# A graph network's last pass picks rows by one-hot products, its first attention pass gets a ring of 28 groups, and its projection stages run three norms ahead

## The reference

```python
h = relu(layernorm(x)); x = x + log_softmax(sage2(h, src, dst))      # two SAGE convolutions
h = relu(layernorm(x)); x = x + gat_ff(h, src, dst)                  # 4 heads, batchnorm, feed-forward
h = relu(layernorm(x)); x = x + gat_prelu(h, src, dst)               # 2 heads
h = relu(layernorm(x))
msg = h[src] @ weight[rel] + bias[rel]                               # 4 relations
agg = where(deg > 0, segment_max(msg, dst), 0)
return x + h @ weight[-1] + bias[-1] + agg
```

## Time and profile before

| what | value |
|---|---|
| median of 3 runs | 5873.08 us |
| the profiled execution's own time | 5876.16 us |
| its span, first to last instruction | 5874.4 us |
| mean granted clock of TensorE | 0.728 |
| TensorE busy | 3278.1 us (56%) |
| VectorE busy | 2906.4 us (49%) |
| ScalarE busy | 1827.9 us (31%) |
| GpSimd busy | 3903.4 us (66%) |

### The profile page before, as it was taken

The page is one execution under the profiler, slowest core; times in us unless marked ns, Lnnn a source line. Parts: engine busy times, 40 slices in busy tenths (PEclk is TensorE's granted clock), DMA queues, the critical chain, the costliest instruction groups (busy, mean ns, idle before and its releaser), DMA issues. The chain is left out here.

```text
span 5874.4 us, 89970 instructions
## 1 busy us (share of the span) xinstructions
PE 3278.1 (56%) x15772; PEld 2756.8 (47%) x15773; DVE 2906.4 (49%) x7625; ACT 1827.9 (31%) x6493; POOL 3903.4 (66%) x4083
## 2 busy tenths in 40 slices
PE   3444555545555525889999894244555563334332
PEld 3444455444555523677777644233445533333331
DVE  4233344434455656788888852344555652222221
ACT  2111111111122213666666653233344441111110
POOL 4777777677777747777776003777777517777776
PEclk9667777766677756999999995566677785555555
DMA  4222222211111112344444211222222134444443
GB/s 122 61 62 63 63 65 66 72 53 52 53 53 52 53 41 78 111 113 117 119 117 113 95 46 31 52 53 54 53 53 52 38 111 130 133 132 130 131 133 107
DMA packets 441899, 474.71 MB, mean 81 GB/s; under 512 B 131954, under 2 KB 337214, under 8 KB 441695
## 3 DMA queue, kind: packets, MB, share of 16 engines
q0 software_dynamic: 130464, 264.37, 17.1%
q1 hardware_dynamic: 184116, 146.31, 8.3%
q10 hardware_dynamic: 127227, 63.09, 3.6%
HBM read 315.46 MB, written 157.97 MB: 81 GB/s over the span
## 5 line engine op out<-in xcount | busy, mean ns | idle before, releaser
L1194 PE MATMUL pa<-arena,weighted 128*128 x4480 | 860.0, 367 | 855.8 <-POOLq L913 511.2
L1194 PEld LDWEIGHTS pa<-arena,weighted 128*128 128x128 f32 x4480 | 795.4, 273 | 909.4 <-issue 909.2
L422 POOL DMA_INDIRECT arena<-y_tab,slot x784 | 739.8, 944 | 398.7 <-issue 209.4
L1607 POOL DMA_INDIRECT arena<-t_tab,src_idx x784 | 777.5, 992 | 265.7 <-issue 216.0
L919 POOL DMA_INDIRECT arena<-h_tab,src_idx x784 | 742.8, 947 | 308.1 <-issue 221.9
L2490 POOL DMA_INDIRECT arena<-t_tab,src_idx x784 | 753.3, 961 | 244.9 <-issue 224.6
L919 POOL DMA_INDIRECT arena<-sage_tab,src_idx x784 | 739.8, 944 | 262.4 <-issue 216.1
L471 DVE TENSOR_TENSOR_SCAN scan_t<-mask,scan_t,pa 128x512 f32<-128x512 bf16 x196 | 250.9, 1280 | 737.1 <-PE pa L495 737.1
L495 PE MATMUL pa<-ident,arena 128*128 128x128 f32 x784 | 218.3, 434 | 603.9 <-DMA arena<-y_tab,slot 603.9
L495 PEld LDWEIGHTS pa<-ident,arena 128*128 128x128 f32 x784 | 140.1, 217 | 681.9 <-DMA arena<-y_tab,slot 430.8
L2731 PE MATMUL pa<-weighted 128*128 128x130 f32 x2240 | 422.6, 364 | 21.0 <-ACT weighted L2809 11.0
(11 more groups left out here) (522 smaller groups left out, 6559.9 us busy)
## 6 DMA issues: line engine op xcount, KB each, us to landing
gat_tab<-out_rows SPq DMA_DIRECT2D x248, 260.0 KB
scan_rows<-out_rows ACTq DMA_DIRECT2D x196, 256.0 KB, 3.7
arena<-t_tab,src_idx POOLq DMA_INDIRECT x1568
mask<-cut_row SPq DMA_DIRECT2D x196, 128.0 KB, 3.1
arena<-h_tab,src_idx POOLq DMA_INDIRECT x784
arena<-sage_tab,src_idx POOLq DMA_INDIRECT x784
y_tab<-arena SPq DMA_DIRECT2D x49, 256.0 KB, 2.3
arena<-y_tab,slot POOLq DMA_INDIRECT x784, 2.8
```

The source lines that it names most:

```text
L422: nc.gpsimd.indirect_dma_start(out=rows(c, t), out_offset=None, in_=table[:, :], in_offset=bass.IndirectOffsetOnAxis(ap=slot[:, c, t:t + 1 ...
L1194: ins = nc.tensor.matmul(pa[:, b * CE:b * CE + RW], hot[b][:, t * P:(t + 1) * P], ring[:, bass.ds(start + t * RW, RW)], start=(t == 0), st ...
L1607: nc.gpsimd.indirect_dma_start(out=rows[:, g % QR * QT + t, :], out_offset=None, in_=t1_tab[:, :], in_offset=bass.IndirectOffsetOnAxis(ap= ...
```

## The change

**Last layer.** `edge_pass`, `gather_results`, `scan_rows` and `last_idx` go. In their place stands a walk of 160 steps over a ring of 8 groups of 7 tiles, filled from y_tab. Step s: ScalarE copies the group from the ring to `staged_t` (`stage_group`), TensorE transposes it (`turn`), VectorE scans 896 edges and carries the last value to the next step where that has the next group (`scan`), TensorE transposes back (`back`), ScalarE copies the result from PSUM (`keep_back`), and TensorE multiplies it by a one-hot matrix that is 1 where an edge is the last of its node (`select`), which puts each node's row on its partition. VectorE adds it to x (`add`), and ScalarE stores the block to the output (`store`); a block that several steps touch is stored by each. Masks are broadcast by ScalarE's queue (`load_mask`). The rows of last edges come from `last_rows`, made in the pass from dst_rows and gathered by group.

**First attention pass.** QR is 28. `arena` and `x` become one tensor `wide`, and the ring lies over x. x is stored to `x_tab` by SP in the projection stage in front of the pass, and loaded in the feed-forward stage behind it, ahead of the additions.

**Fronts.** In stages with `starts`, front(i+2) comes ahead of the wait for product i, as in the others.

**Small.** `group_col1` and `block_col1` keep the first attention pass from overwriting the others; three small operations, a transpose, a few memsets and the load of scan_rows go.

```diff
-QR = 17
+QR = 28
...
     def step(i, b, left):
-        if left > 1 and starts is None:
+        if left > 1:
             front(dve, i + 2)
         dve.wait_ge(group_product.sem, group_product.past(i + 1))
         post(dve, i, b)
-        if left > 1 and starts is not None:
-            front(dve, i + 2)
...
+                sp.dma_start(x_tab[...], x[:, i * NG:(i + 1) * NG, :]).then_inc(stored.sem, 16)
...
+                sp.dma_start(x, x_tab.rearrange("(j p) d -> p j d", p=P)).then_inc(x_here.sem, 16)
...
-        edge_pass(y_tab, D, y_idx, cut_row, ALU.add, ALU.max)
...
+    # SP
+    with sp.Fori(0, GN) as g:
+        n = sp.value_load(retire_walk[0:1, bass.ds(g, 1)], min_val=1, max_val=SN)
+        wait_apart(sp, edge_staged.sem, edge_staged.past(n))
+        sp.sem_inc(group_freed.sem, 1)
+    # VectorE
+    def scan(s, b):
+        after(dve, edge_turned, s + 1)
+        after(dve, mask_loaded[b], (s - b) * 8 + 16)
+        after(dve, edge_back, s - 1)
+        after(dve, carry_ready, s)
+        v.tensor_tensor_scan(run_t[b], mask_t[b], turned_ps[b], carry_t[b], ALU.add, ALU.max).then_inc(edge_scanned.sem, 1)
+        ... (two operations that make carry_t[1 - b])
+    def add(s, b):
+        after(dve, block_summed, s + 1)
+        after(dve, block_added, s)
+        after(dve, block_stored, s * 16)
+        v.tensor_tensor(row, row, last_ps[b], ALU.add).then_inc(block_added.sem, 1)
+    def body(i, b):
+        scan(i, b); build(i, b); add(i - 2, b)
+    # TensorE
+    def turn(s, b):
+        after(pe, edge_staged, s + 1)
+        after(pe, edge_scanned, s - 1)
+        ... (7 transposes of staged_t[b] to turned_ps[b])
+    def back(s, b):
+        after(pe, edge_scanned, s + 1)
+        after(pe, edge_kept, s)
+        ... (7 transposes of run_t[b] to back_ps)
+    def select(s, b):
+        after(pe, edge_kept, s + 1)
+        after(pe, hot_built, s + 1)
+        after(pe, block_added, s - 1)
+        ... (7 matmuls of hot[b] and kept_t[b] to last_ps[b])
+    def body(i, b):
+        turn(i + 1, 1 - b); select(i - 1, 1 - b); back(i, b)
+    # ScalarE
+    def stage_group(s, b, start, need):
+        after(act, edge_turned, s - 1)
+        wait_apart(act, group_landed.sem, group_landed.past(need))
+        nc.scalar.copy(staged_t[b]..., ring[...]).then_inc(edge_staged.sem, 1)
+    def load_mask(s, b, need):
+        after(act, edge_scanned, s - 1)
+        act.dma_start(mask_t[b], cut_row[...].broadcast_to([P, GE])).then_inc(mask_loaded[b].sem, 16)
+    def keep_back(s, b):
+        after(act, edge_back, s + 1)
+        after(act, block_summed, s - 1)
+        nc.scalar.copy(kept_t[b], back_ps).then_inc(edge_kept.sem, 1)
+    def store(s, b, j):
+        after(act, block_added, s + 1)
+        act.dma_start(out[bass.ds(j * P, P), :], x[:, bass.ds(j, 1), :]...).then_inc(block_stored.sem, 16)
+    def body(i, b):
+        keep_back(i, b); store(i - 2, b, j)
+        stage_group(i + 2, b, start, need); load_mask(i + 2, b, need)
```

More of the change, by code:

```diff
@@ L28 @@
 NB = 4
-CHUNKS = ET // CT
-ITERS = CHUNKS // NB
 H1, H2, R = 4, 2, 4
@@ L250, in build @@
         sums_ready = count("sums_ready")
[L252 to L259, removed]
+        iota_made = count("iota_made")
         table_in = count("table_in")
@@ L319, in build @@
         cuts_kept = count("cuts_kept")
[L320 to L325, removed]
+        edge_staged = count("edge_staged")
+        edge_turned = count("edge_turned")
+        edge_scanned = count("edge_scanned")
+        edge_back = count("edge_back")
+        edge_kept = count("edge_kept")
+        carry_held = count("carry_held")
+        carry_ready = count("carry_ready")
+        mask_loaded = [count(f"mask_loaded{b}") for b in range(2)]
         group_staged = count("group_staged")
@@ L564, in results_gathered @@
-        def results_gathered():
-            for b in range(2):
-                group_rows[b].base += 16 * NG * ((groups + 1 - b) // 2)
-            group_here.base += groups
         def stage(s):
@@ L583, in group_steps, with project @@
                 step(i, i % 2, min(groups - 1 - i, 2))
-        def project(ns, front, by_tile, by_group, post, begin=None, scalar_front=None, scalar_post=None, gathers=None, store=None,
+        def project(ns, front, by_tile, by_group, post, begin=None, scalar_front=None, scalar_post=None, store=None,
                     buffers=None, starts=None):
@@ L608, in project @@
             with nc.Block() as block:
-                if gathers is not None:
-                    @block.gpsimd
-                    def _(pool):
-                        gathers(pool)
                 if starts is not None:
@@ L1363, in _ @@
                 few = {"allow_slow_non_contiguous": True}
-                for c in (*hot_made, chunk_scanned, chunk_copied, *written, tile_out, group_kept, *tile_stored):
+                for c in (tile_out, group_kept, *tile_stored):
                     act.sem_inc(c.sem, c.ahead)
@@ L2886, in _ @@
             @block.vector
             def _(dve):
-                with dve.Fori(0, groups) as i:
-                    dve.wait_ge(group_here.sem, group_here.past(i + 1))
-                    nc.vector.tensor_tensor(middle(x, i), middle(x, i), middle(g, i), ALU.add).then_inc(group_kept.sem, 1)
-            @block.sync
-            def _(sp):
-                for i in range(groups):
-                    sp.wait_ge(group_kept.sem, group_kept.past(i + 1))
-                    j, full = i * NG, NG if i < groups - 1 else NG - 1
-                    sp.dma_start(out[j * P:(j + full) * P, :].rearrange("(j p) d -> p j d", p=P), x[:, j:j + full, :]
-                                 ).then_inc(stored.sem, 16)
-                sp.dma_start(out[(NT - 1) * P:N, :], x[0:NL, NT - 1, :]).then_inc(stored.sem, 16)
-                sp.wait_ge(stored.sem, stored.past(16 * (groups + 1)))
+                v = nc.vector
```

393 lines of the change are left out of this document (197 added, 196 removed).

## The result

The changed kernel takes 5946.05 us (median of 4 runs, 5939.82 to 5949.07) against 5872.95 for the kernel before on the same chip: ratio 1.0122, 95% interval 1.0105 to 1.0140: slower, clear of noise and by under 2%. The prediction said 5954 and gave slower a chance of 0.66. The profiled execution took 5939.82 us, with a span of 5938.1 and a mean granted clock of 0.779.

What follows compares the result with a forecast made beforehand. GpSimd's gathers were taken to pace the old last pass; in the new one TensorE and ScalarE alternate. Last pass +110 and fronts -29 give +81 on 5876.2, 5957, or 5954 against the median; range 5820 to 6105 us.

Steps and rivals of the forecast that it cites:

- The ring of two engines: Last pass: TensorE and ScalarE alternate by queue order, so a step costs the sum of both engines' work.
- Its price: One step of the last pass: 5.96 us at full clock, 9.07 at half clock.
- store's issue between the two copies: ScalarE's time for issuing the store between keep_back and stage_group: taken as 0.5 us, bounds 0.1 and 0.7.
- The clock: Last pass: granted clock 0.78 at TensorE busy near 0.63, paired from the earlier windows, giving 7.0 us a step.
- The gathers don't hold it: Last pass: the gather bound of 1136 us lies below the walk's 1168, with gathers priced 1.247 us apart.
- Sum of the pass: Last pass: 42 + 160 x 7.0 + 6 = 1168 us against 1058.4, +110 us.
- Fronts: Two projection stages: earlier fronts save 13 us in the first and 16 in the second, together -29 us.
- Ring of 28, store and load of x: First attention pass: larger ring gives 0 (bounds -25 and 0); moving x costs 0, at most 10 us.
- Full clock: Rival, chance 0.20: clock stays full in the last pass, step 5.96 us, gathers pace the first half; 5833 us.
- half clock: Rival, chance 0.08: half clock throughout the last pass, 9.07 us a step, +412; 6285 us.
- gathers as the sole pace: Rival, chance 0.03: gathers stay the last pass's pace, if the two engines' ring costs under 5.4 us; 5777 us.
- Mask or store late: Rival, chance 0.06: landings over 6 us make the last pass's steps about 8 us, +241; 6115 us.

Runs made afterwards that it cites:

- e3: The changed kernel with ScalarE's stage_group and load_mask moved ahead of keep_back and store; ratio 1.0274 to the kernel before, on a slow chip.
- e7: The changed kernel with TensorE's step reordered to turn, back, select; ratio 1.0235 to the kernel before, on a slow chip.
- e8: The changed kernel with ScalarE's stage copy made twice in each step; ratio 1.0629 to the kernel before, on a slow chip.
- e4: The changed kernel with the one-hot build's row of numbers in PSUM instead of SBUF; ratio 1.0440 to the kernel before, on a slow chip.
- e11: The changed kernel with TensorE's order turn, back, select and the build's row in PSUM; ratio 1.0327 to the kernel before, on a slow chip.
- e1: The kernel before with only the edit putting front(i+2) ahead of the wait for product i; ratio 0.9987 to the kernel before, on a slow chip.
- e2: The changed kernel with the first attention pass's ring back at 17 groups; ratio 1.0412 to the kernel before, on a slow chip.

## Why the prediction was right

- **The ring of two engines: right.** PE waits for the stage copy and ScalarE for back, in turn, as forecast; e3, e7 and e8 show that the order and the copies' length set the step. Of the signs one came only at the end: gathers stopped for the ring twice, 7.4 us in all. The eight slots took up what the walk fell behind until the last two groups.
- **Its price: 0.71 us too high at full clock** (5.25 against 5.96). The term "store's issue between the two copies", taken as 0.5 with bounds 0.1 and 0.7, measured -0.07: a bound from the earlier trace rows that did not hold, because there the issue waited for its copy and here it doesn't. The Trainium skill (TensorE: Matmul & The Clock Gate, Architectural detail) has ScalarE's queue eight deep and strict first in, first out, which allows that overlap; the trace agrees with it, and its case of 6.6 us a step is what the second half shows (6.61). The handoff back to TensorE, 0.23 from the earlier trace rows, measured 0.06 (5564.42 to 5564.48).
- **The clock: right, by a wrong pairing.** 0.77 and 0.78 in both halves against 0.78, but TensorE is 72% busy at 0.75 where the earlier trace rows had 59% at 0.75. The busy share alone doesn't fix the clock: e7 has 1.00 at 73% busy.
- **"The gathers don't hold it": wrong for the first 495 us.** They held 63 steps there, at 7.9 us each. The step of the sum that failed is the gathers' price of 1.247 us: they came 1.34 us apart (1052.4 / 783), as 65 us went into long ones (805.4 - 739.9).
- **Sum of the pass:** 494.4 to 5281, 641 to 5922 and 16.1 to the end are 1151.5, forecast 1168. The cheaper step (some 0.4 x 160 = -64) and the gathers' hold nearly cancel, so part of the hit is luck: with gathers of 1.247 and steps of 6.61 the pass would have come to 48 + 160 x 6.61 = 1106 or the gather bound's 528 + 86 x 6.61 + 6 = 1102, some 45 us less.
- **Fronts: right, -26.3 against -29.** First stage 8.1 against 13: the first post came 3.1 us later than the old (2099.01 against 2098.22 with 2.3 us of lead), forecast 2.5, and the period was 7.3 against 7.4, but the 49 scatters took 66.6 us from first to last (2100.06 to 2166.70), as six of them took 1.33 to 1.87, against 63. (The prediction's last paragraph has posts 9 us apart there, its sum 7.4; the sum was right.) Second stage 18.2 against 16: a period of 10 us against 10.8.
- **Ring of 28, store and load of x: 0, right.** The first attention pass with the feed-forward stage behind it is as long as before within 2 us (above), and the way from the first gather of the second attention pass to that of the last pass took 1151.2 us against 1152.0.
- **Rivals.** Full clock, half clock and gathers as the sole pace didn't happen. Mask or store late: VectorE's scan does wait 323.9 us for the mask's load, 157 times, but under TensorE's select; ScalarE waits only 10.0 us for a scan.

## What to carry to other kernels

Write both engines' queues side by side and follow one item through them: a copy that stands behind a wait for the other engine's last instruction makes the two take turns, whatever is double-buffered, and moving one call in either body takes it out (e3, e7). Price each thing in such a ring from a row where it has the same wait; where there is no such row, let its lower bound be 0. And before a stretch is put down to the chain of waits, check the period ahead of and behind the point at which it changes engines, and whether the engine that it blames was itself waiting there.

## What the runs showed of the hardware

- **A build with two operands in SBUF lengthens a gather's issue.** In the changed kernel 129 of the last pass's 784 gathers take 0.98 to 1.86 us, where the others take 0.944. Of these 129, 126 start while one of VectorE's builds runs, and each is longer by about what the build has left, less 0.1 us: the one at 5563.41 takes 1.61, 0.67 more, and the build had 0.78 us to go. Of the gathers that start ahead of a build and run into it, 96, none is longer. With one operand in PSUM the mean is 944 ns in e4 and none is over 961 ns in e11; e4's longest is 1.29. The Trainium skill (SBUF — State Buffer, SBUF: two separate sides) describes a port pair that a VectorE instruction with two SBUF inputs and a GpSimd instruction that reads SBUF hold in turn, each for its whole length. The gather reads its row numbers from SBUF, and the trace agrees: a gather that starts second is the longer one. The second SAGE pass has the same build with its row in PSUM, and none of its gathers is over 1.08 us.
- **Chips differ in a way that no instruction's duration shows.** Three of them run this kernel 27% slower. In the last pass the standstills come while GpSimd gathers and stop with its last gather: the 12 or 13 steps behind it run at their full pace. One of 10.9 us also falls into the second projection stage, where GpSimd scatters (e1). More time is lost where gathers follow each other more closely (ring of 28: some 34 us; row in PSUM: 83); that this is the reason isn't shown. What is held, whether code, descriptors or something else, no run here shows.
- **The clock went with the pauses, and the busy share didn't tell it.** Behind the last gather, steps of 4.3 to 4.8 us with pauses of up to 1.5 us ran at 1.00 (e7), pauses of 1.95 gave 0.79 (e2) and pauses of 2.99 gave 0.70 (e8). At the same busy share the clock was 1.00 in one run (e7, 73%) and 0.75 in another (the changed kernel at 5300, 72%). A step has the same work in all of them, so a shorter pause is also more work per us, and these runs don't separate the two.
